# A 1024-step recurrence with attention, a quantised FFN, cross-attention and a mixture of experts: three scan elements in the cell, and expert tiles that write their own output rows

## What is computed

```python
def _lstm_cell(x, h, c, Wi, Wh, bi, bh):
    g = x @ Wi.T + bi + h @ Wh.T + bh
    i, f, gg, o = jnp.split(g, 4, axis=-1)
    c2 = jax.nn.sigmoid(f) * c + jax.nn.sigmoid(i) * jnp.tanh(gg)
    h2 = jax.nn.sigmoid(o) * jnp.tanh(c2)
    return (h2, c2)
...
def step(carry, x_t):
    h0, c0, h1, c1, a = carry
    xin = jnp.concatenate([x_t, a], axis=-1)
    h0, c0 = _lstm_cell(xin, h0, c0, Wi0, Wh0, bi0, bh0)
    h1, c1 = _lstm_cell(h0, h1, c1, Wi1, Wh1, bi1, bh1)
    q = h1 @ Wq.T
    attn = jax.nn.softmax(jnp.einsum('bh,bsh->bs', q, context), axis=-1)
    mixed = jnp.einsum('bs,bsh->bh', attn, context)
    a2 = jnp.tanh(jnp.concatenate([mixed, h1], axis=-1) @ Wo.T + bo)
    return ((h0, c0, h1, c1, a2), a2)
...
    t = x.reshape(-1, d)
    logits = t @ switch_w + switch_b
    route_prob = jax.nn.softmax(logits, axis=-1)
    route_prob_max = jnp.max(route_prob, axis=-1)
    routes = jnp.argmax(route_prob, axis=-1)
    for e in range(n_experts):
        h = jax.nn.gelu(t @ w1[e] + b1[e])
        y = h @ w2[e] + b2[e]
        out = jnp.where((routes == e)[:, None], y, out)
    out = out * route_prob_max[:, None]
x = x + _L0_xattn_ref(_layernorm(x), ...)
x = x + _L0_ffn_ref(_layernorm(x), ...)
x = x + _L1_xattn_ref(_layernorm(x), ...)
x = x + _L1_ffn_ref(_layernorm(x), ...)
```

## Time and profile before

| | us |
|---|---|
| median of 3 runs | 8434.98 (8434.35 to 8435.3) |
| the profiled execution | 8436.1 |
| its span | 8434.3 |
| PE busy, share of the span | 81% |
| DVE busy | 50% |
| ACT busy | 38% |
| POOL busy | 3% |

### The profile page before, as it was taken

How to read it: one execution, slowest core, us unless ns; L and a number is a source line. 1 busy time by engine, 2 the same in 40 slices (tenths; PEclk the granted TensorE clock), 3 DMA queues, 4 the chain that set the end, 5 groups by cost and what they waited for, 6 DMA issues and landing times. The chain is left out here.

```text
span 8434.3 us, 813385 instructions
## 1 busy us (share of the span) xinstructions
PE 6828.4 (81%) x380504; PEld 5803.5 (69%) x380505; DVE 4235.9 (50%) x21151; ACT 3225.4 (38%) x15030; POOL 279.8 (3%) x289
## 2 busy tenths in 40 slices
PE   6888888888888888888888888888888888776687
PEld 5777777777777777777777777777777777553454
DVE  5555555554554455455555455545545555565712
ACT  3333333333333333333333333333333333332322
POOL 0000000000000000000000000000000000012501
PEclk8999999999999999999999999999999999888798
DMA  2000000000000000000000000000000000000333
GB/s 85 5 0 0 0 0 0 0 0 0 0 0 0 0 0 0 0 0 0 0 0 0 0 0 0 0 0 0 0 0 0 0 0 0 0 6 18 111 116 112
DMA packets 62186, 95.43 MB, mean 11 GB/s; under 512 B 13633, under 2 KB 50497, under 8 KB 60993
## 3 DMA queue, kind: packets, MB, share of 16 engines
q1 hardware_dynamic: 59072, 86.54, 3.0%
q0 software_dynamic: 3072, 8.39, 0.3%
HBM read 74.99 MB, written 19.92 MB: 11 GB/s over the span
## 5 line engine op out<-in xcount | busy, mean ns | idle before, releaser
L304 PE MATMUL scan_sums<-rec_wh,scan_hT 128*4 128x64 f32 x131008 | 2392.1, 219 | 4.2 <-issue 4.1
L425 DVE STREAM_TRANSPOSE scan_sums<-scan_sums 128x64 f32<-128x64 f32 x6144 | 1546.0, 266 | 1137.6 <-PE scan_sums L304 1137.3
L304 PEld LDWEIGHTS scan_sums<-rec_wh,scan_hT 128*4 128x4 f32 x131008 | 1989.5, 89 | 4.9 <-issue 4.9
L304 PE MATMUL scan_sums<-rec_wa,scan_aT 128*4 128x64 f32 (+1 forms) x65536 | 1104.3, 219 | 382.0 <-ACT scan_aT L385 382.0
L304 PEld LDWEIGHTS scan_sums<-rec_wa,scan_aT 128*4 128x4 f32 (+1 forms) x65536 | 915.4, 88 | 570.9 <-ACT scan_aT L385 570.9
L304 PE MATMUL scan_sums<-rec_wx,scan_xT 128*4 128x64 f32 (+1 forms) x65536 | 1292.1, 219 | 7.7 <-issue 6.8
L304 PE MATMUL scan_sums<-rec_wi,scan_hT 128*4 128x64 f32 (+1 forms) x65536 | 1102.5, 219 | 168.8 <-DVE scan_hT L475 165.2
L304 PEld LDWEIGHTS scan_sums<-rec_wi,scan_hT 128*4 128x4 f32 (+1 forms) x65536 | 913.6, 88 | 357.6 <-DVE scan_hT L475 353.9
L304 PEld LDWEIGHTS scan_sums<-rec_wx,scan_xT 128*4 128x4 f32 (+1 forms) x65536 | 1024.2, 89 | 8.4 <-issue 7.4
L365 ACT ACTIVATE scan_sums<-rec_bias 128x192 f32<-128x192 f32 x2050 | 687.2, 335 | 475.1 <-DVE scan_hT L475 469.5
L370 ACT ACTIVATE scan_tanh_f<-scan_sums 128x8 f32<-128x8 f32 x2048 | 364.1, 178 | 1187.9 <-DVE scan_sums L425 1187.9
(11 more groups left out here) (247 smaller groups left out, 5750.5 us busy)
## 6 DMA issues: line engine op xcount, KB each, us to landing
experts_bias<-in_b SPq DMA_DIRECT2D x40, 640.0 KB, 3.8
moe_w<-in_w SPq DMA_DIRECT2D x16, 1024.0 KB, 12.3
slots_x<-route_zero SPq DMA_DIRECT2D x40, 128.0 KB, 1.7
experts_x<-slots_x SPq DMA_DIRECT2D x40, 128.0 KB, 2.1
slots_y<-experts_y SPq DMA_DIRECT2D x40, 128.0 KB, 1.7
w_xres<-in_x_steps SPq DMA_DIRECT2D x8, 512.0 KB, 11.3
w_xres<-in_x SPq DMA_DIRECT2D x4, 1024.0 KB, 11.7
out<-w_xres SPq DMA_DIRECT2D x8, 512.0 KB, 3.0
```

Of the source, the lines that this page charges most:

```text
L304: last = nc.tensor.matmul(sums[layer][BANK[g]][32 * j:32 * j + ROWS[g], 0:64], state[:, k, FIRST[g]:FIRST[g] + ROWS[g]], weight[:, k, j, 6 ...
L425: nc.vector.transpose(turned[l][g], sums[l][g][:, 0:64]).then_inc(gates_turned[l][g], 1)
```

## The change

In the cell, the scan has three elements per unit (24 in all) with the operators multiply, then add, and the constants 0 and 1. Its third element is twice the new cell value. ACT halves it inside the tanh's scale, writes that tanh to bank O instead of F, and copies the halved cell value into a new SBUF tile `c[l]` that the forget term reads in the next step.

In the experts, each slot row gets two more columns (`ROW` = 258): the token's number and the reciprocal that is its route probability. Unused slots hold a token number that is out of bounds. POOL writes the numbers at the start of `route`. At the end of SP's part of `route`, x is stored to a DRAM tensor `x_rows` by four DMAs of 1 MB. In `experts`, DVE casts a tile's token numbers, POOL fetches the x rows of the tile by an indirect DMA, DVE's `finish` multiplies by the probability and adds the x rows, and POOL writes the tile's rows to `out` by an indirect DMA. The wait for `x_rows` stands in POOL's program of `experts`, ahead of the first fetch. SP's store of the tile, `slots_y` and the whole of `gather` are gone. SP's x load of a tile now also waits for `y_done`.

```diff
+ROW = D + 2
+NOBODY = float(2 * B * T)
...
-        scanned = [m.sbuf(f"scanned{l}", [P, 2, 2, B, 4]) for l in range(2)]
+        scanned = [m.sbuf(f"scanned{l}", [P, 2, 2, B, 3]) for l in range(2)]
...
-        cell = [sums[l][F][:, 256:288] for l in range(2)]
-        tanh_c = [sums[l][F][:, 288:296] for l in range(2)]
-        c_of = [t.rearrange("p (v e) -> p v e", e=4)[:, :, 3] for t in cell]
+        cell = [sums[l][F][:, 256:280] for l in range(2)]
+        tanh_c = [sums[l][O][:, 288:296] for l in range(2)]
+        twice_c = [t.rearrange("p (v e) -> p v e", e=3)[:, :, 2] for t in cell]
+        c = [m.sbuf(f"c{l}", [P, 2 * B]) for l in range(2)]
...
-                        nc.scalar.activation(tanh_c[l], c_of[l], ACT.Tanh).then_inc(h_factors[l], 1)
+                        nc.scalar.activation(tanh_c[l], twice_c[l], ACT.Tanh, scale=0.5).then_inc(h_factors[l], 1)
+                        nc.scalar.activation(c[l][:], twice_c[l], ACT.Copy, scale=0.5).then_inc(c_kept[l], 1)
                         seed(l, n + 1)
...
-                        nc.vector.scalar_tensor_tensor(forget_term[l], tanh_f[l][:].rearrange("p k b -> p (k b)"), 1.0, c_of[l],
+                        nc.vector.scalar_tensor_tensor(forget_term[l], tanh_f[l][:].rearrange("p k b -> p (k b)"), 1.0, c[l][:],
                                                        ALU.add, ALU.mult).then_inc(c_terms[l], 1)
...
-                        nc.vector.tensor_tensor_scan(cell[l], flat[l][:, 0], flat[l][:, 1], 0.0, ALU.add, ALU.mult).then_inc(c_done[l], 1)
+                        nc.vector.tensor_tensor_scan(cell[l], flat[l][:, 0], flat[l][:, 1], 0.0, ALU.mult, ALU.add).then_inc(c_done[l], 1)
...
+                for b in range(B):
+                    sp.dma_start(x_rows[b].rearrange("(g p) d -> p g d", p=P), xres[:, :, b, :]).then_inc(w["x_kept"], 16)
                 sp.wait_ge(filled, 16 * SLOT_TILES)
...
                     sp.wait_ge(x_turned_done, n)
+                    sp.wait_ge(y_done, n)
                     sp.dma_start(x[b][:], slots_x[bass.ds(g * B * P + P * b, P), :]).then_inc(x_in[b], 16)
-                    sp.wait_ge(y_done, n)
...
-                def store(g, b):
-                    sp.wait_ge(y_done, number(g, b) + B)
-                    sp.dma_start(slots_y[bass.ds(g * B * P + P * b, P), :], y[b % 2][:]).then_inc(stored[b % 2], 16)
-                in_steps(sp, [(store, 4), (load, 0)], GROUPS)
+                in_steps(sp, [(load, 0)], GROUPS)
...
+                pool.wait_ge(w["x_kept"], 16 * B)
+
+                def fetch(g, b):
+                    n = number(g, b)
+                    pool.wait_ge(token_done, n)
+                    pool.wait_ge(y_done, n + 2)
+                    nc.gpsimd.indirect_dma_start(before[b % 2][:], None, x_rows, bass.IndirectOffsetOnAxis(ap=token[b][:], axis=0),
+                                                 bounds_check=B * T - 1, oob_is_err=False).then_inc(before_in[b % 2], 16)
+
+                def put(g, b):
+                    pool.wait_ge(y_done, number(g, b) + B)
+                    nc.gpsimd.indirect_dma_start(out_rows, bass.IndirectOffsetOnAxis(ap=token[b][:], axis=0), y[b % 2][:], None,
+                                                 bounds_check=B * T - 1, oob_is_err=False).then_inc(stored[b % 2], 16)
+                for n in range(SLOT_TILES + 1):
+                    if n < SLOT_TILES:
+                        fetch(n // B, n % B)
+                    if n > 0:
+                        put((n - 1) // B, (n - 1) % B)
...
+                    dve.wait_ge(x_in[b], 16 * g + 16)
+                    nc.vector.tensor_copy(token[b][:], x[b][:, D:D + 1]).then_inc(token_done, 1)
                     dve.wait_ge(h_turned_done, 2 * n)
...
-                    nc.vector.tensor_tensor(y[b % 2][:], y_sum[:, 0:D], bias[b][:, FF:FF + D], ALU.add).then_inc(y_done, 1)
+                    nc.vector.tensor_tensor(y[b % 2][:], y_sum[:, 0:D], bias[b][:, FF:FF + D], ALU.add).then_inc(biased, 1)
+                    dve.wait_ge(before_in[b % 2], seen(g, b))
+                    dve.wait_ge(biased, number(g, b))
+                    nc.vector.scalar_tensor_tensor(y[b % 2][:], y[b % 2][:], x[b][:, D + 1:D + 2], before[b % 2][:],
+                                                   ALU.mult, ALU.add).then_inc(y_done, 1)
```

More of the change, by code:

```diff
@@ L1104, in _, with route @@
                 in_steps(pool, [(weigh, 2)])
-def route(nc, ins, xres, xn, slot, expert, prob, slots_x, w):
+def route(nc, ins, xres, rows, slot, expert, slots_x, x_rows, w):
     with ExitStack() as ctx:
@@ L1151, in _ @@
             def _(pool):
-                nc.gpsimd.memset(zero[:], 0.0).then_inc(zeroed, 1)
+                nc.gpsimd.memset(blank[:, 0:D], 0.0).then_inc(zeroed, 1)
+                nc.gpsimd.memset(blank[:, D:ROW], NOBODY).then_inc(zeroed, 1)
+                nc.gpsimd.iota(token[:], [[P, NB], [T, B]], base=0, channel_multiplier=1).then_inc(tokens_kept, 1)
+                pool.wait_ge(tokens_kept, 1)
+                nc.gpsimd.tensor_copy(rows[:, :, D], token[:].rearrange("p g b -> p (g b)")).then_inc(tokens_kept, 1)
                 nc.gpsimd.memset(before[:], 1.0).then_inc(const, 1)
@@ L1252, in _ @@
                 then(nc.vector.tensor_reduce(total[:], exps[:], AX.X, ALU.add), 7)
-                then(nc.vector.reciprocal(prob[:], total[:]), 8)
+                then(nc.vector.reciprocal(rows[:, :, D + 1], total[:]), 8)
                 dve.wait_ge(counted, 1)
@@ L1281, in _, with scatter @@
                 then(nc.vector.tensor_copy(expert[:], expert_f[:]), k + 15)
-def scatter(nc, xn, slot, slots_x):
+def scatter(nc, rows, slot, slots_x):
     sent = Pool(nc, None, "scatter").sem("sent")
@@ L1291, in _, with experts @@
                 nc.gpsimd.indirect_dma_start(slots_x, bass.IndirectOffsetOnAxis(ap=slot[:, n:n + 1], axis=0),
-                                             xn[:, n // B, n % B, :], None).then_inc(sent, 16)
+                                             rows[:, n, :], None).then_inc(sent, 16)
             pool.wait_ge(sent, 16 * NT)
-def experts(nc, ins, expert, slots_x, slots_y, w):
+def experts(nc, ins, expert, slots_x, x_rows, out_rows, w):
     with ExitStack() as ctx:
         m = Pool(nc, ctx, "experts")
-        x = [m.sbuf(f"x{i}", [P, D]) for i in range(B)]
+        x = [m.sbuf(f"x{i}", [P, ROW]) for i in range(B)]
+        token = [m.sbuf(f"token{i}", [P, 1], I32) for i in range(B)]
+        before = [m.sbuf(f"before{i}", [P, D]) for i in range(2)]
         xT = m.sbuf("xT", [P, KC, P])
@@ L1311, in experts @@
         stored = [m.sem(f"stored{i}") for i in range(2)]
+        before_in = [m.sem(f"before_in{i}") for i in range(2)]
+        token_done, biased, cleared = m.sem("token_done"), m.sem("biased"), m.sem("cleared")
         x_turned_done, xT_done, h_sum_done, h_done, gelu_done, h_turned_done, hT_done, y_sum_done, y_done = (
@@ L1517, in build @@
             m = Pool(nc, ctx, "moe")
-            w = {"ident": ident, "w1": m.sbuf("w1", [P, E, KC, FF]), "w2": m.sbuf("w2", [P, E, FC, D]), "loaded": m.sem("loaded")}
+            w = {"ident": ident, "w1": m.sbuf("w1", [P, E, KC, FF]), "w2": m.sbuf("w2", [P, E, FC, D]), "loaded": m.sem("loaded"), "x_kept": m.sem("x_kept")}
             slot = m.sbuf("slot", [P, NT], I32)
             expert = m.sbuf("expert", [P, SLOT_TILES], I32)
-            prob = m.sbuf("prob", [P, NT])
             with ExitStack() as routing:
-                xn = Pool(nc, routing, "moe").sbuf("xn", [P, NB, B, D])
-                route(nc, ins, xres, xn, slot, expert, prob, slots_x, w)
-                scatter(nc, xn, slot, slots_x)
-            experts(nc, ins, expert, slots_x, slots_y, w)
-            gather(nc, xres, slot, prob, slots_y, out)
+                rows = Pool(nc, routing, "moe").sbuf("rows", [P, NT, ROW])
+                route(nc, ins, xres, rows, slot, expert, slots_x, x_rows, w)
+                scatter(nc, rows, slot, slots_x)
+            experts(nc, ins, expert, slots_x, x_rows.rearrange("b t d -> (b t) d"), out.rearrange("b t d -> (b t) d"), w)
 def lay_out(inputs):
```

67 lines of the change are left out of this document (24 added, 43 removed).

## The result

| | before | after |
|---|---|---|
| median, us | 8434.67 (8430.61 to 8435.3, 4 runs) | 8345.18 (8343.51 to 8346.82, 4 runs) |
| ratio | | 0.9895, 95% interval 0.9881 to 0.9909 |
| profiled execution | 8436.1 | 8346.82 |
| its span | 8434.3 | 8345.0 |

The kernel is 1.05% faster, 89.5 us. The prediction was 8354 with a range of 8338 to 8380: 9 us too high, inside the range.

The account below looks back on a forecast made before the run. The serial recurrence, 7.25 of 8.43 ms, was taken as the bound, with everything from the scan on serial. Terms -35.5 + 0 + 11.1 + 0 - 57.2 = -81.6 us gave 8354, range 8338 to 8380.

Parts of the forecast that it names:

- The scan: Cell's scan, 32 to 24 elements: 17.3 ns less each, 35.5 us over 2048 scans.
- The back-to-back pair of rows (11.0): Alternative scan estimate from scans following back to back, 207 against 174 ns: 11.0 ns saved per scan, 22.5 us.
- rival (a): Cell gives less: 11.0 ns per scan gives 8367, longer forget term up to 8390; chance 0.22, beyond 8390 another 0.05.
- The cell's total: Recurrence over all cells: 35.5 us saved, all from the scan; copy and forget term counted 0.
- two arrows 0.01 apart: At the scan's start: I/G tanh ends at 8.26, O turn at 8.25, so 0.01 of slack.
- 34 as its sign: Recurrence steps: 7.05 us each; the prediction is wrong if they are not 34 ns shorter.
- The copy of c and the forget term from SBUF: In the cell: copy covered between tanh(cell) and the seed (cover 0.10), forget term not longer; cost 0.
- The route's SP queue: End of route: four x_rows issues of 2.92 us make SP last, scatter 11.1 us later (bounds 1.1 and 14.5).
- Rival (b): End of route: x's DMAs find room, SP isn't last; shift 1.1, time 8344; chance 0.12.
- Experts: Expert tiles: longer finish, fetch and put all fit beside PE's tile of about 8 us; sum 0.
- Rival (c): Experts: POOL's fetch and put become the bound, slower; decides from 5.0 us per indirect DMA against 1.26; chance 0.05.
- The end: After the last bias add: put lands at 8376.8, program ends 0.3 later; 57.2 us saved (bounds 56 to 58).

Follow-up runs that it names:

- f1: Changed kernel with a neutral fourth element put back into each unit of the scan, new operators and order of writing kept: 8390.48 us.
- f3: Changed kernel without the ACT copy of c, the forget term reading 2c straight from PSUM (+1 and halving left out): 8346.84 us.
- e3: Changed kernel with the four transfers of x's rows issued by SP in the scatter block instead of in route: 8325.63 us, ratio 0.9878.
- e4: Changed kernel with SP instead of POOL waiting for the last writes of rows: 8336.09 us, ratio 0.9891.
- f4: Changed kernel with POOL and DVE each waiting for the last write, then clearing 8 elements of an own tile: 8348.65 us (one run).
- g3: Changed kernel without the writes of rows of the last two expert tiles, the waits lowered to match: 8338.34 us (one run).

## Why the prediction was right, and where only by luck

- **The scan**: right in mechanism and size. 233 to 217 ns, 16 against 17.3 forecast from the scan that doesn't follow another one, and tanh(cell) earlier by the same amount: 251 instead of 267 ns behind the scan's start on average. The back-to-back pair of rows (11.0) would have been wrong, and so was its rival (a). ("On an idle engine" says too much of the row of 226: it starts 0.04 behind the end of another instruction.) f1 shows that the operators have no part in it. From what the Trainium skill states ("DVE: opcode table, instruction layouts, handler registers and perf-mode slots", Datapath and trigger behaviour), that the scan runs at half throughput, the estimate was 16.7; the trace agrees, with its 16.
- **The cell's total**: mis-sized, 51.5 us instead of 35.5. The step that failed is the start of the scan. The prediction saw two arrows 0.01 apart, took the O turn's for as good as binding and looked for losses there; the binding one was the I/G tanh, and the change had altered its write pattern: from distances of four elements to three. Its duration stands in no term of the sum; it was left as it was without a reason. It gave 8 ns a cell, 16 us (f1). Over all cells the distance from the I/G tanh to the scan fell by 9.6 ns and that from the scan to tanh(cell) by 16.0, 25.6 of the 25.2 measured in all. The steps are 50 ns shorter where the prediction named 34 as its sign.
- **The copy of c and the forget term from SBUF**: 0, right by f3. The cover was there: copy and tanh overlap (starts 0.07 apart).
- **The route's SP queue**: right. 2.85 us per issue against 2.92, and SP in DVE's place as the last; scatter 12.0 later against 11.1. The 0.9 beyond the forecast are for the most part SP's issues ahead of these, which end 0.5 us later than before, and a step from SP's end to the scatter of 1.67, where DVE's had been 1.35. e3 shows that 11.1 of the 12.0 were to be had back. Rival (b), that SP isn't last, falls.
- **Experts**: right at 308.8 us for 39 tiles; the start of the first tile wasn't, by 2.3 us of clock.
- **Rival (c)**, POOL as the bound, falls: a fetch and a put take 1.02 + 0.30 each, 2.7 of 8 us. It was not put to a hard test, though: in the rows of a tile, POOL's issues and DVE's instructions don't lie at the same time (8106.27 DVE's end, 8106.93 put, 8109.29 fetch's end, 8109.55 next DVE instruction), and none of the 80 issues of that trace overlaps a DVE instruction. So these runs say nothing against the trap that the Trainium skill describes ("SBUF — State Buffer", SBUF: two separate sides).
- **The end**: mechanism right, size off: 11.0 us behind the last bias addition instead of 3.8. The step that failed is "program end 0.3 later, as now": as now, SP was the last engine; with the change it is POOL, and its end takes 6.8, of which 6.6 are the `DRAIN` behind 80 indirect transfers. The put starting 0.83 behind the product rather than 0.2 makes up the rest.

That the total is right within 9 us is in part luck: the cell gave 16 us more than forecast, while the end gave 7 less, the scatter cost 1 more and the first load and tile 3. With the size of each known it would have been 8354 - 16 + 7 + 1 + 3 = 8349, less 2.5 us in pieces that the change doesn't touch: 8346.

## What to carry to other kernels

When two arrows meet at an instruction, ask of both whether the change alters anything of them, the layout they write included; here a small ACT instruction got 8 ns shorter by closer output elements at equal size, and 10 more when it wrote them in pairs. Ask which engine will be the last one after a change and read the cost of its end, not that of the engine that is last now; for POOL, that is the `DRAIN` row of a block with a known number of indirect transfers. DMA issues whose landing nobody awaits still cost their issue time (here 2.85 us each, behind sixteen of 1 MB) when a barrier of all engines follows; put them behind the barrier, where the queue engine is idle.

## What the runs showed of the hardware that I had not expected

- A tanh of 128x16 from PSUM to SBUF takes 201 or 200 ns with output elements four apart, 193 with three apart, and 183 as adjacent pairs three apart (in the last case the order of reading had changed too, and its share isn't known).
- The program ends 6.8 to 6.9 us after POOL's last instruction when POOL is the last engine (e4, f4), 0.3 after DVE's when DVE is (g3). POOL's `DRAIN` at the end of a block took 2.66 to 2.68 us behind 32 indirect transfers, 6.46 behind 78 and 6.58 behind 80.
- TensorE's granted clock, as the mean of a stretch, went back from 0.93 to 0.64 in the stretch after its first rise. Ahead of that stretch it had been busy for 1.64 of 4 us; in before the same gap (1.65 of 4) was not followed by a fall (windows above). What decides stays open.
